# Linear attention's memory and state products in two row halves of four heads, one output bank per half

## The reference, cut to what matters

```python
sq, sk = elu1(q), elu1(k)                                  # 16 heads of 16 dims
out_m = jnp.einsum('bhsd,mhde->mbhse', sq, memories)       # 4 memories
rel = jnp.einsum('bhsd,mhd->mbhs', sq, memory_norms)
out_m = out_m / jnp.clip(rel, EPS, None)[..., None]
weights = jax.nn.softmax(rel.mean(axis=-1), axis=0)
mem_out = jnp.einsum('mbhse,mbh->bhse', out_m, weights)
kv_cum = jnp.cumsum(jnp.einsum('bhsd,bhse->bhsde', sk, v), axis=2)
num = jnp.einsum('bhsd,bhsde->bhse', sq, kv_cum)
den = jnp.clip(jnp.einsum('bhsd,bhsd->bhs', sq, jnp.cumsum(sk, axis=2)), EPS, None)
out = g * mem_out + (1.0 - g) * (num / den[..., None])
```

## Time and profile before

| | |
|---|---|
| median of 3 runs | 2573.48 us (2570.85 to 2573.53) |
| profiled execution | 2577.14 us, span 2575.0 us |
| busy | PE 80%, PEld 52%, DVE 65%, ACT 54%, POOL 40% |
| mean granted PE clock | 0.907 |
| HBM | 80.43 MB read, 41.94 MB written |

### The profile page before, as it was taken

How to read it: one execution, slowest core, us unless ns; L and a number is a source line. 1 busy time by engine, 2 the same in 40 slices (tenths; PEclk the granted TensorE clock), 3 DMA queues, 4 the chain that set the end, 5 groups by cost and what they waited for, 6 DMA issues and landing times.

```text
span 2575.0 us, 54488 instructions
## 1 busy us (share of the span) xinstructions
PE 2062.8 (80%) x18018; PEld 1343.3 (52%) x18018; DVE 1682.8 (65%) x4298; ACT 1397.4 (54%) x2758; POOL 1040.8 (40%) x914
## 2 busy tenths in 40 slices
PE   0667888888898888889888787988888887988666
PEld 0435555555555555555556555555655555565333
DVE  6636666767677676766767676676667676776242
ACT  1333555656565564656556465655656565655434
POOL 0424254452625354252535436153544526253211
PEclk9776998989898998989899898989989898999878
DMA  2101324242132324222131413214241421313030
GB/s 85 50 19 52 55 60 66 51 67 58 34 53 59 59 51 67 59 44 51 50 59 51 75 51 58 52 35 59 59 67 51 67 58 37 52 56 50 17 50 9
DMA packets 127440, 135.39 MB, mean 53 GB/s; under 512 B 23056, under 2 KB 108176, under 8 KB 127120
## 3 DMA queue, kind: packets, MB, share of 16 engines
q1 hardware_dynamic: 116368, 114.58, 23.8%
q10 hardware_dynamic: 10752, 16.78, 1.7%
HBM read 80.43 MB, written 41.94 MB: 48 GB/s over the span
## 4 chain that ended last, share of the span: by engine, by line
issue 44%; POOL 18%; PE 14%; DVE 8%; DMA 7%; ACT 4%; SPq 4%; POOLq 1%; ACTq 0%; DVEq 0%
POOL place L615 5%; DMA kst<-scratch 5%; POOL place L605 5%; POOL place L626 3%; PE bank L1288 3%; PE bank L1348 2%; POOL bsl L630 2%; SPq L505 2%; PE bank L1242 2%; POOL place L651 2%; DMA scratch<-place 2%; ACT place L716 2%; DVE mxs L1176 1%; ACT place L719 1%; PE bank L1301 1%
## 5 line engine op out<-in xcount | busy, mean ns | idle before, releaser
L1176 DVE TENSOR_REDUCE mxs<-bank 128x1 f32<-128x128 f32 (+3 forms) x1024 | 429.1, 484 | 216.7 <-PE bank L1437 216.7
L829 ACT ACTIVATE place<-bank 128x512 f32<-128x512 f32 (+1 forms) x768 | 348.4, 540 | 225.3 <-PE bank L1451 224.3
L590 POOL TENSOR_TENSOR rstd<-ve,halfc 128x4 f32<-128x4 f32 x64 | 64.9, 1015 | 677.9 <-DVE ve L945 677.9
L615 POOL TENSOR_TENSOR place<-am,place 128x512 f16<-128x512 f32 x256 | 290.6, 1156 | 111.7 <-ACT place L731 105.6
L731 ACT ACTIVATE place<-am 128x512 f16<-128x512 f32 x256 | 151.8, 625 | 237.3 <-DVE am L1004 237.3
L1435 PE MATMUL bank<-kst,qst 96*128 96x128 f16 (+3 forms) x1024 | 239.0, 305 | 48.3 <-DMA kst<-scratch 33.1
L1449 PE MATMUL bank<-qst,kst 128*128 128x512 f16 (+3 forms) x1024 | 236.9, 303 | 34.5 <-DMA qst<-nmt 19.2
L1301 PE MATMUL bank<-w2q,place 128*128 128x256 f16 x2048 | 250.8, 277 | 10.3 <-POOL place L605 5.5
L1301 PEld LDWEIGHTS bank<-w2q,place 128*128 128x128 f16 x2048 | 200.1, 99 | 46.5 <-issue 7.2
L1242 PE MATMUL bank<-ident,place 128*128 128x128 f32 x512 | 118.0, 390 | 124.8 <-ACT place L686 124.3
L626 POOL TENSOR_TENSOR place<-place 128x512 f16<-128x512 f32 x64 | 84.0, 1316 | 330.7 <-ACT place L755 329.7
(11 more groups left out here) (160 smaller groups left out, 4517.5 us busy)
## 6 DMA issues: line engine op xcount, KB each, us to landing
scratch<-place SPq DMA_DIRECT2D x256, 128.0 KB, 2.4
qst<-scratch SPq DMA_DIRECT2D x256, 64.0 KB, 2.3
kst<-scratch SPq DMA_DIRECT2D x256, 64.0 KB, 2.4
qst<-scratch SPq DMA_DIRECT2D x128, 128.0 KB, 5.2
kst<-scratch SPq DMA_DIRECT2D x128, 128.0 KB, 5.8
xa<-x SPq DMA_DIRECT2D x16, 512.0 KB, 3.5
xc<-xb ACTq DMA_DIRECT2D x16, 512.0 KB, 2.9
out<-xc ACTq DMA_DIRECT2D x16, 512.0 KB, 3.6
```

Of the source, the lines that this page charges most:

```text
L615: G.tensor_tensor(alp[:, n % 2, k, :], am[:, k, :], ahp[:, n % 2, k, :], ALU.subtract).then_inc(s["al"], 1)
L829: A.activation(pf[h % SLOTS][:, S2_COL[k]:S2_COL[k] + S2_W[k]], bank_of(L2, ("S2", h, k))[:, 0:S2_W[k]], ACT.Exp, scale=D ** -0.5 / RS ** ...
L1176: V.tensor_reduce(mxs[:, g:g + 1], bank_of(L2, ("S1", n, k))[:, Q_AT[i]:Q_AT[i] + (i + 1) * P], AX, ALU.max).then_inc(s["mx"], 1)
```

## The change

The block diagonal operands are stored as two row halves: rows 0 to 63 hold heads 0 to 3 of a half, rows 64 to 127 heads 4 to 7, each with columns for its four heads alone. The memory, state and state-sum matmuls are issued in pairs, one for each half: memories and states as 64-row matmuls into two banks (`OU`, r = 0 and 1), the state sums as matmuls with 64 output rows each. A bank now holds everything of four heads: 4 memories x 4 heads x 17 columns, and two local terms (high and low, each 4 x 17; the low term's seventeenth column is a second one for the denominator, since `vp` has 34 columns a head, the last of each 17 being one). A tile uses two banks instead of three. In `outputs` the memory matmuls come first and start the banks' accumulation, then states, then the wait for the low part (`NA`), then local matmuls. `combine` does two clips against a tensor `limits`, one reciprocal and one coefficient product of 48 numbers a row, and two products of 6 x 64 columns. Head blocks are built by more and smaller instructions in the set-up. The table of marks has new numbers throughout.

```diff
@@ jobs1
-            jobs += [(("LO", n), "t6", 3 * n + 3)]
-            jobs += [(("ME", n, k), "t6", 3 * n + k + 1) for k in range(2)]
+            jobs += [(("OU", n, r), "t6", 2 * n + r + 1) for r in range(2)]
@@ sizes
-VW = 2 * D + 1
+VW = 2 * (D + 1)
+QH = HH8 // 2
+BLK = QH * VW
+TERMS = M + 2
+MEMW = M * QH * MW
...
-        bmh = sb("bmh", [P, KH, M, HH8, MW], F16)
+        bmh = sb("bmh", [P, KH, M, QH, MW], F16)
@@ MARKS, lane 1
...
-            "N": [101.8, 105.3, 113, 119.4, 123.9, 129.3, 133.2, 0, 4.8, 10.5],
+            "N": [101.6, 103.7, 110.5, 117.4, 122.4, 127.3, 131.4, 0, 1.7, 10.7],
@@ DVE, combine
-                dve.wait_ge(s["om"], due(L1, "om", t, 3 * n + 1))
-                V.tensor_scalar(den[:, r, M, :], local[:, :, 2 * D], MEM_EPS * AS, None, ALU.max).then_inc(s["clip"], 1)
-                for k in range(2):
-                    dve.wait_ge(s["om"], due(L1, "om", t, 3 * n + 2 + k))
-                    V.tensor_scalar(den[:, r, 2 * k:2 * k + 2, :],
-                                    pairs[k].rearrange("p (m h w) -> p m h w", m=2, w=MW)[:, :, :, D],
-                                    MEM_EPS, None, ALU.max).then_inc(s["clip"], 1)
...
+                for r in range(2):
+                    dve.wait_ge(s["om"], due(L1, "om", t, 2 * n + r + 1))
+                    V.tensor_tensor(den[:, b, r, :, :], outs[r][:, :, :, D], limits[:, :, :],
+                                    ALU.max).then_inc(s["clip"], 1)
...
-                for k in range(2):
-                    V.tensor_tensor(t6[:, r, 2 * k:2 * k + 2, :].rearrange("p m (h d) -> p (m h) d", d=D),
...
+                for r in range(2):
+                    V.tensor_tensor(t6[:, b, :, r * PARTS:(r + 1) * PARTS].rearrange("p t (h d) -> p t h d", d=D),
+                                    outs[r][:, :, :, 0:D],
+                                    coef[:, b, r, :, :].rearrange("p t (h o) -> p t h o", o=1)
+                                    .broadcast_to([P, TERMS, QH, D]), ALU.mult).then_inc(s["t6"], 1)
@@ PE, outputs
-                local = take(L1, ("LO", n), t)
+                into = [take(L1, ("OU", n, r), t) for r in range(2)]
+                halves = [slice(r * PARTS, (r + 1) * PARTS) for r in range(2)]
+                local = [bank[:, MEMW:MEMW + BLK].rearrange("p (t h w) -> p h t w", t=2, h=QH) for bank in into]
+                for m, (a, b) in enumerate(((qh, bmh), (ql, bmh), (qh, bml))):
+                    for r in range(2):
+                        T.matmul(into[r][:, 0:MEMW], a[halves[r]],
+                                 b[halves[r], half, :, :, :].rearrange("p m h w -> p (m h w)"),
+                                 start=(m == 0), stop=(m == 2), skip_group_check=True)
                 if c:
                     state = 3 * half + c - 1
-                    for m, (a, b) in enumerate(((qh, bsh), (ql, bsh), (qh, bsl))):
-                        T.matmul(local[:, 0:HH8 * VW], a, b[:, state, :], start=(m == 0), stop=(m == 2),
-                                 skip_group_check=True)
+                    for a, b in ((qh, bsh), (ql, bsh), (qh, bsl)):
+                        for r in range(2):
+                            T.matmul(local[r], a[halves[r]],
+                                     b[halves[r], state, :].rearrange("p (h t w) -> p h t w", h=QH, t=2),
+                                     start=False, stop=False, skip_group_check=True)
                 yield at1("NA", n + 1)
                 pe.wait_ge(s["al"], due(L1, "al", t, 2 * n + 2))
                 for h in range(HH8):
+                    r, i = divmod(h, QH)
                     for part in (ahp, alp):
...
-                ins.then_inc(s["om"], 1)
-                for k in range(2):
-                    into = take(L1, ("ME", n, k), t)
...
+                    if i == QH - 1:
+                        ins.then_inc(s["om"], 1)
@@ PE, state sums
                         for part in range(2):
-                            ins = T.matmul(into[:, 0:HH8 * VW], skt[:, cc, 2 * half + part, :],
...
+                            for r in range(2):
+                                dims, heads = slice(r * PARTS, (r + 1) * PARTS), half * HH8 + r * QH
+                                ins = T.matmul(into[dims, 0:BLK], skt[:, cc, 2 * half + part, dims],
+                                               L1.vp[:, cc, heads:heads + QH, :].rearrange("p h w -> p (h w)"),
```

More of the change, by code:

```diff
@@ L135 @@
+            "FTT": [24.9],
+            "UP": [28.7, 29.7, 30.6, 31.6, 33.4, 35.1, 36.9, 38.7],
+            "DN": [38.8, 47.1],
+            "DM": [39.7, 40.8, 41, 41.3, 41.5, 41.7, 42, 43],
+            "TT": [67.9],
+            "PA": [75.3, 78.9, 81.3, 83.5],
+            "V": [89.1, 92.8],
+            "SK": [96.6, 96.9, 97.1],
+            "RM": [97.9],
+            "ST": [99.4, 99.5, 100.3, 100.6, 100.8, 101],
         },
@@ L185 @@
[L185 to L193 removed]
+            "TT": [6.7],
@@ L1414, in lane1_start @@
                         for part in range(2):
-                            ins = T.matmul(into[:, 0:HH8 * VW], skt[:, cc, 2 * half + part, :],
-                                           L1.vp[:, cc, half * HH8:(half + 1) * HH8, :].rearrange("p h w -> p (h w)"),
-                                           start=(cc == 0 and part == 0), stop=(cc == c and part == 1))
+                            for r in range(2):
+                                dims, heads = slice(r * PARTS, (r + 1) * PARTS), half * HH8 + r * QH
+                                ins = T.matmul(into[dims, 0:BLK], skt[:, cc, 2 * half + part, dims],
+                                               L1.vp[:, cc, heads:heads + QH, :].rearrange("p h w -> p (h w)"),
+                                               start=(cc == 0 and part == 0), stop=(cc == c and part == 1),
+                                               skip_group_check=True)
                     ins.then_inc(s["st"], 1)
```

280 lines of the change are left out of this document (136 added, 144 removed), and 18 rows, old and new, of the table MARKS.

## The result

The changed kernel takes 2589.3 us (median of 4 runs, 2587.5 to 2595.1) against 2572.5 us (2570.9 to 2573.5) for the kernel before on the same chip: ratio 1.007, interval 1.0052 to 1.0087. It is slower by 0.7%, where 2542 us were forecast. The sign is wrong, and the time is outside the range.

A forecast was written before the change was run, and what follows sets the result against it. Bound by a chain through DVE, then after 1097 us by a full PE with POOL close behind. Terms -10 + 1 - 22 = -31 us take 2577.1 to 2546, median of runs 2542; range 2510 to 2568.

The forecast's parts named there:

- (a): Around 1075 us, PE turns the keys ahead of PV[3], so the turning of heads starts sooner: -0.3 us a trip.
- (d): At the loop's start DVE's masks come first and lane 2's norm 1.2 us later: +0.6 us a trip.
- the clock rival: PE does less where it waits, so its granted clock falls from 0.84 to 0.70: 2568 to 2575 us, chance 0.07.
- Ahead of the loop: Lane 1's lone tiles get shorter, -10 us (bounds -3 and -14); more set-up instructions cost +1 us.
- Per trip: In the loop, four terms sum to -1.6 us a trip, x 14 = -22 us.
- (b): At 1091.67 us, PE's products need only the first DVE product, and outputs are shorter: -1.0 us a trip.
- (c): From 1097 us PE is full; five tiles save 0.35 us each, half counted because of POOL: -0.9 us a trip.
- Scattered writes: State and local matmuls writing 17-column runs take k times the streaming; at k = 4, 2600 us; chance 0.08.
- Lane 2 sets the trip: Lane 2's norm, feed-forward and POOL low parts keep their length; -0.2 us a trip and lone runs stay: 2561 us, chance 0.14.

The follow-up runs named there:

- e1: The changed arithmetic with the old order table (MARKS of the kernel before): 2540.4 us, ratio 0.9874 to the kernel before.
- e4: The changed kernel with, on PE alone, lane 1's products of tiles 0 and 1 issued behind lane 2's output projection: 2552.8 us, ratio 0.9925.
- e7: The changed arithmetic in the old table, with lane 1's query and key steps at the new, later marks on every engine but PE: 2591.5 us, ratio 1.0063.
- e9: The changed kernel with old marks for lane 1's query and key steps, values, stack transposes, memory sums and states: 2603.7 us, ratio 1.0107.
- e10: The changed kernel with lane 1's query and key steps early and products of tiles 0 and 1 behind lane 2's output projection: 2581.7 us, ratio 1.0029.
- e14: The changed arithmetic in the old table, memory matmuls issued twice only in lane 1's first batch, ahead of the loop: 2503.2 us, ratio 0.9717.
- e11: The changed arithmetic in the old table, both products from tile 3 on waiting for both scalings of the tile before last: 2552.5 us, ratio 0.9909.
- e6: The changed arithmetic in the old table, with each of the memories' six matmuls issued twice in every tile: 2533.8 us, ratio 0.9843.
- e17: Repeat of the changed arithmetic in the old table with the memories' six matmuls issued twice in every tile: 2535.1 us, ratio 0.9854.
- e18: The changed arithmetic in the old table, with 48 two-column matmuls added on PE ahead of the loop: 2517.4 us, ratio 0.9758.

## Why the prediction was wrong

The step that failed is one sentence: "Everything from lane 1's feed-forward to lane 2's attention keeps its length". For lane 2's attention it held (its end 101.8 us into the trip for 101.3). For lane 1's queries and keys it did not: in that stretch their steps move later on four engines, POOL's first low part of the keys from 85.3 us into the trip to 91.1, and the sum had no term for it. I had read the moved marks of the tiles and of the loop's start only. Behind these steps stands the path by way of GpSimd, scratch and DMA to the products, where PE now waits 2.85 us a trip, and behind the products lane 2's output projection, whose last group starts 5 us later than before. The prediction's own rule, to ask what is queued behind a wait, was not applied there. Shown: the table costs 49 us against the old one with the same arithmetic (e1), the loss stands ahead of the projection's last group, and 36 of the 49 us come back when nothing of the projection stands behind the keys' wait (e4). Late steps alone can lose as much (e7), by another path. Not settled: how the table's other moves share the rest, as parts of two tables don't add (e9, e10), and how much of each difference is of the kind that e14 shows.

Point by point, against e1:
- **The sum**, without the two terms that belong to the new order, (a) and (d), gives 2538 for the arithmetic; 2540 was measured (2537 when repeated). That is close in part by luck: what precedes the loop moves such a kernel by up to 34 us (e14). The spread was given too small: the terms' bounds, added straight, reach from 2496 to 2583 and not from 2518 to 2565, and the clock rival's +1.5 a trip and +3 give 2566, below the 2568 to 2575 stated.
- **Ahead of the loop**: -10 and +1 forecast; the first store came 12.3 us earlier (13.1 in the changed kernel). The bound was -14. In the changed kernel the 11 tile distances of the lone runs add up to 45.7 us, from 57.5: 11.8 less, where 9.4 were forecast. They range from 3.7 to 5.2, not from 4.1 to 4.3. The coefficient still ends with POOL's first low part (at 103.36, and at about 103.3 as the first of the two from 102.14), but from there to the next masks it is 1.17 us and not the 1.38 of the prediction, which added up durations of instructions that overlap.
- **Per trip**: -1.6 forecast, -1.9 of it for (b) and (c); -2.1 measured in e1 (147.9 to 145.8), of which -2.7 behind the projection and +0.6 ahead of it.
- **(a) Turning of the heads**: in the trip shown it starts 2.3 us after the attention by values ends (1075.74 to 1078.06), for 2.6 before: the 0.3 forecast. No run isolates what it is worth.
- **(b) Earlier products**: -1.0 a trip; undoing them costs 1.0 (e11), though the term was meant to hold the shorter outputs as well, and 1.0 is less than e14 moves a trip.
- **(c) PE full after 1097**: open. Half of PE's 0.35 us a tile was to count, 0.9 a trip; giving the memories' share back costs 0.0 for the trip as a whole and 0.6 behind the projection (e6, e17), with another clock and another start of the loop. How the 2.1 us divide between banks, VectorE and PE's time is not shown.
- **(d) The loop's start**: mis-sized. +0.6 forecast with a norm 1.2 us late. The masks did come first (3.1 us after the trip's start, 6.4 before), but the norm's statistics start 4.3 us after it, as before, and PE's transposes of lane 2 9.2 us after it, where it was 9.1:

```profile
977.37 1.29 DVE L1019 SCALAR_TENSOR_TENSOR am<-bank,tri 128x512 f32<-128x512 f32 x2 [2.39 <-PE bank L1331]
978.57 1.39 DVE L953 BATCH_NORM_STATS2 stats<-xb 128x6 f32<-128x256 f32 x4
...
983.51 1.95 PE L1254 MATMUL bank<-ident,place 128*128 128x128 f32 x7 [1.81 <-ACT place L691]
```

- **Scattered writes**, the rival on the slower side, is refuted, though the sign came out its way. Two state pairs of 136 columns take 0.13 us, by which k is 1.15 at most, and the 16 local matmuls 0.57 against 0.56. The Trainium skill says in "PSUM — Partial Sum Buffer", Specifications, that any non-contiguous AP slows matmuls significantly. For these runs of 17 columns of f32 the measurement does not bear that out.
- **The clock** took nothing back: 0.903 for 0.907 over the span, and 0.92 for 0.84 in 1076:1097.
- **Lane 2 sets the trip** came nearest in kind: over these kernels the trip follows the end of lane 2's output projection, with 35.4 to 37.1 us behind it in all runs that have the new arithmetic. But the projection and what stood ahead of it is a place that this rival did not name.

## What to carry to other kernels

When a change brings a new order with it, price the order and the arithmetic apart, and read every moved row, those far from the edit first: for each step that moves later, go down to its last consumer (here by DMA), and ask what is queued behind that one on its engine. A table of orders is one piece: half of it can be slower than either (e9: 2604 us, 2540 and 2589 with a whole table). The new arithmetic in the old order is 1.3 to 1.4% faster than before, and 2.8% with e14's extra matmuls ahead of the loop; a difference of a per cent between two orders of a software-pipelined loop can also come from what precedes the loop, so look at the length of each trip before giving it a cause.

## What was not expected of the hardware

- Identical loop code ran at 143.3, 145.0 or 144 to 146 us a trip, with other work of PE ahead of the loop (e14, e18, e1).
- With 24 us more of PE's busy time in the span the kernel was no slower, and the granted clock rose from 0.906 to 0.919 (e6).
- Matmuls write runs of 17 columns with next to no loss: 0.065 us a pair of 64-row matmuls of 136 columns (L1355), where half of the 0.115 of a 272-column pair is 0.057, and 0.025 us a step of 34 columns in the 128-row ones (L1363), as for 33 in one piece in the kernel before.
